# Two-layer transformer block on one core: the second layer's first batch is ranked ahead of its scores, part of its work moves into the first layer's tail, and 12 idle products follow the first layer's last product

## The reference

```python
xn = _layernorm(x)                       # x is layer 0's output
# attention over the 512 tokens of a batch, one head of 128 channels
k = xn @ Wk.T + bk; q = xn @ Wq.T + bq; v = xn @ Wv.T + bv
attn = softmax(q @ k.T / sqrt(128), axis=1)
a = attn @ v / sqrt(128)
# mixture of 8 experts, 2 per token, on rms_norm(xn)
scores = rms_norm(xn) @ w_router.T
scores_topk, idx = top_k(scores, 2); weights = softmax(scores_topk)
# each token's two rows go through their experts: up, u * silu(gate), down
x = x + a + (xn + sum_k weights_k * down_k)
```

## Time and profile before

| | |
|---|---|
| median of 3 runs | 596.63 us (596.29 to 597.83) |
| profiled execution: its own time | 594.71 us |
| profiled execution: span, first to last instruction | 593.0 us |
| outside the span (594.71 - 593.0) | 1.7 us |
| layer 1's attention and routing, from the boundary to the first expert product | 354.2 to 462.3 us |
| mean granted TensorE clock | 0.956 |

### The profile page before, as it was taken

How to read it: one execution, slowest core, us unless ns; L and a number is a source line. 1 busy time by engine, 2 the same in 40 slices (tenths; PEclk the granted TensorE clock), 3 DMA queues, 4 the chain that set the end, 5 groups by cost and what they waited for, 6 DMA issues and landing times. The chain is left out here.

```text
span 593.0 us, 17933 instructions
## 1 busy us (share of the span) xinstructions
PE 518.5 (87%) x6023; PEld 331.4 (56%) x6023; DVE 440.7 (74%) x1874; ACT 363.0 (61%) x1073; POOL 298.3 (50%) x326
## 2 busy tenths in 40 slices
PE   6378998999989999989899869989987999999991
PEld 5124344444444444445444445666657899999991
DVE  6698888798797987978887337999985376565652
ACT  2163787777777777777777757876752345444441
POOL 5580844826447164462000113888786276666662
PEclk9665999999999999999999988999998999999997
DMA  3947155282462734717300506111112234445442
GB/s 90 208 108 127 39 140 113 75 172 64 128 144 70 165 77 125 145 34 167 76 23 19 161 20 261 52 47 41 47 58 79 61 104 122 140 133 155 133 118 79
DMA packets 51098, 61.04 MB, mean 103 GB/s; under 512 B 9969, under 2 KB 41845, under 8 KB 49408
## 3 DMA queue, kind: packets, MB, share of 16 engines
q1 hardware_dynamic: 45536, 50.13, 34.1%
q0 software_dynamic: 4320, 8.47, 4.3%
q10 hardware_dynamic: 1152, 1.31, 0.7%
HBM read 31.68 MB, written 28.39 MB: 101 GB/s over the span
## 5 line engine op out<-in xcount | busy, mean ns | idle before, releaser
L666 DVE CUSTOM_DVE_ANT_0 A<-A,band 128x320 f32<-128x320 f32 (+2 forms) x512 | 213.4, 466 | 44.3 <-PE A L838 43.3
L521 ACT ACTIVATE Pb<-SB 128x320 f32<-128x320 f32 (+2 forms) x512 | 179.6, 402 | 75.8 <-PE SB L874 71.4
L838 PE MATMUL A<-Ks,Qs 48*64 48x320 bf16 (+2 forms) x1024 | 129.5, 304 | 18.5 <-DVE mneg L666 15.0
L865 PE MATMUL SB<-Qs,Ks 50*64 50x320 bf16 (+2 forms) x1024 | 131.7, 294 | 4.8 <-ACT Pb L521 4.2
L838 PEld LDWEIGHTS A<-Ks,Qs 48*64 48x64 bf16 x1024 | 48.1, 106 | 117.8 <-DVE mneg L666 91.4
L1714 POOL DMA_INDIRECT results<-y,xt x71 | 75.2, 1060 | 51.0 <-issue 35.6
L874 PE MATMUL SB<-ends,ident 64*64 64x64 bf16 (+1 forms) x1024 | 99.8, 205 | 1.2 <-issue 1.2
L887 PE MATMUL PV<-Pb,Va 128*32 128x320 f32 (+2 forms) x1024 | 85.6, 406 | 0.4 <-ACT Pb L521 0.4
L1820 PE MATMUL l_S<-xT,wt 128*128 128x128 f32 x568 | 82.0, 287 | 1.1 <-ACT xT L1722 1.1
L1820 PEld LDWEIGHTS l_S<-xT,wt 128*128 128x128 f32 x568 | 68.7, 191 | 8.6 <-ACT xT L1722 1.5
L1189 POOL DMA_INDIRECT expert_rows<-pay,pos x64 | 62.7, 980 | 19.9 <-issue 17.9
(11 more groups left out here) (249 smaller groups left out, 858.6 us busy)
## 6 DMA issues: line engine op xcount, KB each, us to landing
Qs<-parts_dram SPq DMA_DIRECT2D x14, 384.0 KB, 5.8
Ks<-parts_dram SPq DMA_DIRECT2D x14, 384.0 KB, 9.2
xt<-expert_rows SPq DMA_DIRECT2D x71, 65.0 KB, 2.0
yb<-results SPq DMA_DIRECT2D x8, 512.0 KB, 4.1
parts_dram<-qp SPq DMA_DIRECT2D x16, 192.0 KB, 2.8
parts_dram<-kp SPq DMA_DIRECT2D x14, 192.0 KB, 2.8
xb<-in_x SPq DMA_DIRECT2D x8, 256.0 KB, 2.9
parts_dram<-qp SPq DMA_DIRECT2D x16, 128.0 KB, 2.6
```

The lines of the kernel that those rows point to most:

```text
L521: act.activation(Pb[:, group % 4, c, 0:w], SB[k % NB_BANKS][:, 0:w], ACT.Exp).then_inc(act_exp, 1)
L666: nc.vector.tensor_tensor_reduce(scores_of, scores_of, band[:, skip:skip + w], -1.0, 3e38, ALU.add, ALU.min, mneg[:, step % 2, col:col + 1 ...
L838: mm = nc.tensor.matmul(A[k % NA_BANKS][out:out + HP, 0:w], Qs[b % RING][rows, a, HP * sub:HP * sub + HP], Ks[b % RING][rows, a, lo:lo + w ...
L865: nc.tensor.matmul(out[r0:r0 + HP, 0:w], Ks[b % RING][rows, a, HP * sub:HP * sub + HP], Qs[b % RING][rows, a, lo:lo + w], start=True, stop ...
```

## The change

- Layer 0's tail on ACT goes on behind `evac_ctxT(7)` with `rows_of(0)`, `squares(1)` and `arg_1(1)` (new function `tail_rows`), which stood at the start of layer 1's `run`.
- `pay` is allocated with layer 1's own tiles, ahead of layer 0, so that the tail can write it.
- In layer 1's batch 0, PE does `rank(0)` ahead of `turn(1)` and the scores, DVE does `ranks(0)` and `route_b(0)` ahead of the maxima, and ACT does `gate_exp(0)` ahead of `evac_xnT(1)` and the exponentials. Batches 1 to 7 keep their order.
- PE issues 12 idle f32 products of 128 columns (`WARM_TAIL`) behind `out_mm(7)`, before the boundary.

```diff
+WARM_TAIL = 12
@@ layer0, ACT
-        follow["act"](act)["tail"]()
+        tail = follow["act"](act)
+        tail["tail"]()
         evac_ctxT(NB - 1)
+        tail["tail_rows"]()
@@ layer0, PE
         out_mm(NB - 1)
+        for i in range(WARM_TAIL):
+            nc.tensor.matmul(A[0][:, 0:P], ident[:], ident[:], start=True, stop=True)
@@ layer1
+    pay = [sb(f"pay{i}", [P, TOPK, NT, ROW]) for i in range(2)]
@@ layer1, ACT
-        def run():
-
+        def tail_rows():
+
+            rows_of(0, 0, 0)
             squares(1)
             arg_1(1)
-            rows_of(0, 0, 0)
+
+        def run():
             for g in range(NB):
                 p, last = g % 2, g == NB - 1
-                if last:
+                if last or g == 0:
                     gate_exp(g)
-                else:
+                if not last:
                     evac_xnT(g + 1)
...
                 if not last:
                     evac_q(g + 1, 1 - p)
-                    gate_exp(g)
+                    if g > 0:
+                        gate_exp(g)
@@ layer1, DVE
-                if last:
+                ranks_first = last or g == 0
+                if ranks_first:
                     ranks(g, last)
-                    rows_to_pad()
+                    if last:
+                        rows_to_pad()
                     route_b(g, p)
...
-                if not last:
+                if not ranks_first:
                     ranks(g, last)
...
-                    route_b(g, p)
+                    if not ranks_first:
+                        route_b(g, p)
@@ layer1, PE
-                if last:
+                if last or g == 0:
                     rank(g, p, last)
-                else:
+                if not last:
                     turn(g + 1)
...
-                if not last:
+                if not last and g > 0:
                     rank(g, p, last)
```

More of the change, by code:

```diff
@@ L1104, in layer1 @@
     Sb = XR = QK = OU = XV = RT = QB = KB = blocks = None
-    pr = vs = pay = x2b = tab = w_up = w_dn = after = None
+    pr = vs = x2b = tab = w_up = w_dn = after = None
     def value_blocks(bank):
@@ L1114, in tail_banks, with attach @@
         XV, QB, KB, blocks = turned[:, 0:512], q_bank, k_bank, value_blocks(v_banks)
-    def attach(banks, pr_, vs_, pay_, x2b_, tab_, w_up_, w_dn_, after_):
-        nonlocal Sb, XR, QK, OU, XV, RT, QB, KB, blocks, pr, vs, pay, x2b, tab, w_up, w_dn, after
+    def attach(banks, pr_, vs_, x2b_, tab_, w_up_, w_dn_, after_):
+        nonlocal Sb, XR, QK, OU, XV, RT, QB, KB, blocks, pr, vs, x2b, tab, w_up, w_dn, after
         Sb, XR, QK, OU = banks
         XV, RT, QB, KB, blocks = XR[:, 0:512], XR[:, 512 + 2 * (P + NE):1024], QK, QK, value_blocks(XR)
-        pr, vs, pay, x2b, tab, w_up, w_dn, after = pr_, vs_, pay_, x2b_, tab_, w_up_, w_dn_, after_
+        pr, vs, x2b, tab, w_up, w_dn, after = pr_, vs_, x2b_, tab_, w_up_, w_dn_, after_
     CNT = 64
@@ L1306, in run @@
             after["act"](act)
-        return {"tail": tail, "run": run}
+        return {"tail": tail, "tail_rows": tail_rows, "run": run}
     def dve_part(dve):
@@ L1862, in build @@
             pr = ctx.enter_context(nc.sbuf_tensor("l1_pr", [P, NT, T], F32))
-            pay = [ctx.enter_context(nc.sbuf_tensor(f"pay{i}", [P, TOPK, NT, ROW], F32)) for i in range(2)]
-            follow["attach"](banks, pr, vs, pay, x2b, tab, w_up, w_dn, after)
+            follow["attach"](banks, pr, vs, x2b, tab, w_up, w_dn, after)
             block = ctx.enter_context(nc.Block())
```

## The result

| | before | after |
|---|---|---|
| median of 20 runs each, beside one another | 596.10 us (592.84 to 599.95) | 592.18 us (590.37 to 597.11) |
| ratio after / before | | 0.9939, 95% interval 0.9920 to 0.9957 |
| profiled execution: its own time | 594.71 us | 591.76 us |
| profiled execution: span | 593.0 us | 590.0 us |
| granted clock, mean | 0.956 | 0.958 |

The kernel is faster by 0.61% (2.6 to 4.8 us by the interval). Medians are over all runs; ratios leave out single runs more than 1.5% above the fastest of their kernel, among them five of 1105 to 1506 us on chips 0, 7 and 14. The predicted mechanism is there step by step, and the sum for the profiled execution (591.7) came out at 591.76.

What follows compares the result with a forecast made beforehand. POOL was taken to bound the kernel through scatter(0)'s start: 3.38 us gained there, 3.0 left after scatter(1)'s wait, boundary and slow transfers priced at zero, so 596.63 - 3.0 = 593.6 us, range 592.6 to 595.6.

Steps and rivals of the forecast that it cites:

- What bounds the kernel: POOL, never waiting for data after 366.48 us: each microsecond that scatter(0) starts earlier is one off the total.
- The boundary: Between layers 0 and 1: moved ACT work ends at 353.4, idle products 354.0, SP's drain 354.1; price zero.
- rival 3: Clock drops before or in the idle products, boundary 2.7 us late: 2.2 us slower, 598.9; chance 0.05.
- The clock: Layer 1's start: clock full, as idle products shrink PE's gap and a 1.07 us gap elsewhere kept it full.
- Batch 0: Layer 1's first batch: scores take 3.60 us, roots(1) starts at 361.22, scatter(0) at 363.10 instead of 366.48; gain 3.38 us.
- Rival 1: Clock low all the same at layer 1's start: scatter(0) gains 1.1 us, the total 0.45, 596.2; chance 0.13.
- Rival 4: POOL's start: roots(1) was not the wait, so only 1.37 us goes; within Rival 1's price, no own chance.
- rival 2: scatter(1) starves or transfers are slow under the weight loads: gain 1.7 to 2.2 us, 594.4 to 594.9; chance 0.14.
- Scatter(1) late next: Batch 1: its scatter waits for route_b(1), starting at 375.31 to 375.55, before 378.50; gain left 3.0 us.
- Batch 2 on: Later batches: POOL has 0.7 us of slack, DVE and PE needing some 11.2 us a batch, POOL 11.85.
- The sum: Whole profiled execution: 594.71 - 3.0 = 591.7 us.
- The median: Median of runs: 1.9 us above the profiled execution, so 596.63 - 3.0 = 593.6 us.

Runs made afterwards that it cites:

- e11: The changed kernel plus one spare POOL root (1.62 us) ahead of scatter(4): 595.09 us beside 595.70 for the kernel before, ratio 0.9998.
- e12: The kernel before plus only the 12 idle products: 592.90 us beside 595.70 for the kernel before, ratio 0.9954.
- e17: The changed kernel without idle products (new order and moved ACT work alone): 594.52 us beside 595.27 for the kernel before, ratio 0.9981.
- e18: The changed kernel with 24 idle products instead of 12: 594.85 us beside 595.27 for the kernel before, ratio 0.9993.
- e16: The changed kernel with 5 idle products instead of 12, on chip 14: ratio 1.0002 to the kernel before.
- e10: The changed kernel with the short chain (ranks, positions, statistics, next argument) first in every batch: 590.86 us beside 595.70 for the kernel before, ratio 0.9938.
- e13: The changed kernel without idle products, on chip 14: ratio 1.0045 to the kernel before.
- e2: The changed kernel without idle products, on chip 12: ratio 1.0002 to the kernel before.
- e6: The changed kernel without idle products, on chip 13: ratio 1.0034 to the kernel before.
- e14: The changed kernel, unaltered, on chip 14: ratio 0.9996 to the kernel before.
- e9: The changed kernel, unaltered, compared a second time with the kernel before, on chip 7: 592.07 us beside 595.70, ratio 0.9950.

## Why the prediction was right or wrong

**What bounds the kernel: right on this kind of chip.** e11 shows it by adding to POOL (1.0 of 1.6 us arrived at the experts), e12 and e17 by starting it sooner. On chips 12 to 14 it does not hold.

**The boundary: right.** The tail's last ACT step began at 353.21, the idle products ended at 351.23 + 2.84 = 354.07 (354.0 predicted), and layer 1's first product stands at 354.46, where the kernel before had 354.48. SP's drain was the last one (354.2). The price of rival 3 is real: e18, 2.6 us for 12 products more.

**The clock: right in effect.** 1.00 throughout. In all 14 profiles with 12 or 24 idle products the scores of batch 0 take 3.60 us, in the five with none 4.66 to 5.59. The argument from the pause of 1.07 us was thin, since the clock does not go by the length of a pause (last section); e16 held at 1.95.

**Batch 0: right to 0.1 us.** Last step of the positions 356.81 (356.8 predicted), statistics 359.31 (359.33), `arg_0(2)` 360.85 (360.78), roots(1) 361.31 (361.22), first transfer 363.14 (363.10). The split of the 3.38 us, 2.25 through the clock and 1.1 through the removed wait, is in the table: roots(1) comes 2.29 us sooner, and scatter(0) follows it 1.18 us closer. The parts alone gave 2.39 and 1.26.

**The rivals.** Rival 1's price is e17's and rival 3's that of e18, but neither happened: the clock held and the idle products ended in time. Rival 4 falls with the row of roots(1), which still is what the first transfer waits for (0.19 us behind it).

**Slow transfers (rival 2): right at zero, nearly.** The first transfer took 1.30 us in place of 1.24, the next seven the usual 0.95 to 0.96:

```profile
L1196 POOL DMA_INDIRECT expert_rows<-pay,pos x64: 955/959/1300, 363.1 to 454.0; - x64
```

That is the earlier trace rows again. The Trainium skill (SBUF — State Buffer, the "DVE blocks DMA" trap and the section on a bandwidth pool below it) gives 3100 ns for a GpSimd-issued transfer beside a DVE copy; none of the 64 held POOL for more than 1300.

**Scatter(1) late next: right.** Positions of batch 1 end their last step at 375.03 (374.83 and up to 0.24 more), the transfer follows at 375.49 (375.31 to 375.55), with the short wait for `pay` that was named. Its cause in the sum was right as well: DVE's four maxima of batch 1 each wait 0.17 to 0.20 us for PE.

**Batch 2 on: right, with too much slack.** "POOL has 0.7 us of slack, since DVE and PE need some 11.2 us a batch": the rows of DVE show 11.41 and 11.45 where it waits for nothing from POOL. The slack is 0.4 us a batch; nothing came of the difference here.

**The sum: right, 591.7 against 591.76.** That it fits to 0.1 us is luck: from roots(0) to the first expert product the gain is 3.24 us (114.49 to 111.25) and not 3.0, but layer 0 took 0.13 us longer in the profile of after and the experts 0.11.

**The median: wrong.** The step that failed is "The median is 1.9 above that execution, so the forecast is 596.63 - 3.0", and with it the low end. The 1.9 was the offset of a median of three. Over 20 runs, these three among them, the median is 596.10, so 1.4 above; on chips 7 and 0 it was 595.70 and 595.27. The changed kernel's median lies 0.4 above its own profiled execution. With 596.10 the same gain gives 593.1, and the low end of the range moves from 592.6 to 592.1, under the measured 592.18: the base of 596.63 alone put it outside. What remains, 0.9 us, is inside what the medians can tell: the ratio allows 2.6 to 4.8, the second comparison 1.4 to 4.6, and the profiles give 3.2 and 3.4 from roots(0) to the first expert product (114.49 against 111.25 and 111.14). The low end had room for "0.6 of scatter between runs", while single executions of either kernel spread over some 7 us (592.84 to 599.95, 590.37 to 597.11).

**Where that spread comes from.** In 20 profiles roots(0) starts between 347.15 and 352.04, with the same instructions ahead of it. Two executions, of after and then of e12, by PE's timeline and by windows, at one place of layer 0, which the change does not touch:

```profile
97.06 0.24 PE L877 MATMUL SB<-ends,ident 64*64 64x128 bf16 x2 [0.35 <-issue]
```

```profile
99.42 0.24 PE L875 MATMUL SB<-ends,ident 64*64 64x128 bf16 x2 [3.02 <-issue]
```

```profile
100.00:105.00 5.00, 4.55 (x73) 2.02 (x69) 4.90 (x24) 3.52 (x11) 2.05 (x5) 1.00 0.02 3
```

```profile
100.00:105.00 5.00, 4.79 (x56) 2.02 (x52) 2.94 (x15) 2.41 (x8) 0.00 (x0) 0.69 0.01 3
```

The same product is issued 2.36 us later, for no releaser that the profile has, and the clock falls behind the pause (0.69). A POOL step (L391) that starts at 106.38 in after starts at 110.18 in e12, so 3.8 of the 4.1 us between the two roots(0) are there by then. That this standstill makes up the spread of the times is argued from 20 profiles; only the places are shown.

## What to carry to other kernels

A start moved sooner is worth what the second-latest chain leaves of it: read its period where it does not wait (11.4 beside 11.85 us here, 11.65 in the order of e10) and its end at the next stage before believing more. Idle products that bridge a pause are worth the slow work behind it (2.4 us here) as long as they end before the drain that was last anyway; 12 beyond delayed the next stage by 2.6 us, 0.22 each. And price a median from the sum of one profile only with the spread of single executions, taking a median of three as uncertain by a microsecond.

## What the runs showed of the hardware

- **The clock doesn't go by the length of the pause.** The order-only kernel has the same pause ahead of layer 1 in four profiles (3.06 to 3.08 us), and the clock fell 1.3 us into it on one chip (e13), 1.1 on another (e17), 2.8 in e2, and in e6 only at 356.5, 1.1 us after the pause had ended at 355.37. Windows of e13, then of e6:

```profile
353.00:354.00 1.00, 0.00 (x0) 0.00 (x0) 0.90 (x5) 0.97 (x8) 0.00 (x0) 0.70 0.00 0
```

```profile
356.00:357.00 1.00, 1.00 (x5) 0.68 (x4) 0.90 (x6) 0.60 (x1) 0.00 (x0) 0.74 0.36 113
```

  It stayed at 1.00 through 1.95 us in e16, and through 3.73 us ahead of the last output product in e10. At the same place it fell 0.9 us behind the end of a pause of 3.43 in the changed kernel, and 1.1 us ahead of the end of one of 3.42 in e12. Windows of the changed kernel, then of e12, then of e10:

```profile
445.00:446.00 1.00, 1.00 (x7) 1.00 (x7) 0.97 (x2) 0.67 (x2) 0.83 (x1) 0.52 0.43 133
```

```profile
453.00:454.00 1.00, 1.00 (x7) 1.00 (x7) 0.35 (x2) 0.00 (x0) 0.69 (x2) 0.50 0.20 68
```

```profile
445.00:446.00 1.00, 1.00 (x11) 1.00 (x11) 0.97 (x2) 0.74 (x2) 0.69 (x2) 1.00 0.25 78
```

The output product took 5.47, 6.57 and 3.84 us. In e12 (and e18, 6.48) it came so late that the 72 idle products behind it, and not POOL, held the first expert product: the 0.9 us that e12 lost between the last transfer and that product. The Trainium skill (TensorE: Matmul & The Clock Gate, Part 1) calls the gate's window free-running and the number of slow products at a start run-variable. The trace agrees: one kernel's scores took 5.29, 5.44 and 5.59 us in e6, e17 and e13.

- **One kernel, two speeds by chip**: 595 to 596 us on chips 0 and 7, 633 to 637 on 12 to 14. The span of e14 is 43.1 us longer than that of e9, and 37.2 of these lie between roots(0) and the first expert product, where ACT and DVE wait for releases that the profile can't name. The cause stays open.
